# Attention items of two heads with both kinds of attention, row-paired score and maxima matmuls, and softmax division moved to the last stage

## The reference

```python
qkv = x @ qkv_w + qkv_b                              # q, k, v of 16 heads x 16 channels
std_logits = q . k * 16 ** -0.5                      # kind DOT
write_lines = exterior(x_prev @ w1_write, x @ w2_write)   # 6 numbers per head, unit length
read_lines = exterior(x @ w1_read, x @ w2_read)
geo_logits = (read_lines . J write_lines) * inc_scale     # kind GEO, 6 channels
std_out = softmax(causal(std_logits)) @ v
geo_out = softmax(causal(geo_logits)) @ (x @ geo_w + geo_b)
gate = mean(sigmoid(x @ gate_w + gate_b))
x = layernorm(x + ((1 - gate) * std_out + gate * geo_out) @ out_w + out_b)
x = layernorm(x + (silu(x @ w_gate) * (x @ w_up)) @ w_down)   # hidden 768, int weights / 127
```

## Time and profile before

| | us |
|---|---|
| median of 3 runs (lowest, highest) | 2109.17 (2107.64, 2111.22) |
| span of the profiled execution | 2112.1 |
| stage project / attend / finish in it | 241 / 1525 / 346 |
| busy PE, ACT, DVE, POOL | 1930.6, 1273.4, 1129.4, 336.9 |

### The profile page before, as it was taken

The page is one execution under the profiler, slowest core; times in us unless marked ns, Lnnn a source line. Parts: engine busy times, 40 slices in busy tenths (PEclk is TensorE's granted clock), DMA queues, the critical chain, the costliest instruction groups (busy, mean ns, idle before and its releaser), DMA issues. The chain is left out here.

```text
span 2112.1 us, 35917 instructions
## 1 busy us (share of the span) xinstructions
PE 1930.6 (91%) x11400; PEld 769.0 (36%) x11400; DVE 1129.4 (53%) x2179; ACT 1273.4 (60%) x1641; POOL 336.9 (16%) x609
## 2 busy tenths in 40 slices
PE   8888498999998999999899999989999995899998
PEld 4444122333332333333233333323333322556555
DVE  5666377565564655556465655646565403443442
ACT  4555544577776777677677767767777783222121
POOL 3333303111211110111111011111101111000000
PEclk9999699999999999999999999999999997999999
DMA  6668660404133250414324041432500004112000
GB/s 192 205 211 254 163 107 25 86 21 90 37 70 46 50 86 6 91 20 73 49 47 86 6 91 21 72 46 50 86 6 30 4 11 103 43 51 65 20 20 20
DMA packets 138525, 145.83 MB, mean 69 GB/s; under 512 B 46784, under 2 KB 120768, under 8 KB 136288
## 3 DMA queue, kind: packets, MB, share of 16 engines
q1 hardware_dynamic: 137136, 140.32, 30.4%
q0 software_dynamic: 624, 2.75, 0.4%
q10 hardware_dynamic: 576, 0.28, 0.1%
HBM read 88.25 MB, written 54.53 MB: 68 GB/s over the span
## 5 line engine op out<-in xcount | busy, mean ns | idle before, releaser
L931 ACT ACTIVATE prob<-ex 128x1024 f32<-128x1024 f32 (+2 forms) x1280 | 1074.5, 893 | 444.4 <-PE ex L776 438.8
L946 DVE TENSOR_REDUCE mp<-mx 128x1 f32<-128x512 f32 (+3 forms) x1280 | 749.2, 609 | 547.4 <-PE mx L794 287.5
L776 PE MATMUL ex<-qa,ka 98*128 98x512 bf16 (+3 forms) x2560 | 675.6, 354 | 62.7 <-issue 28.3
L827 PE MATMUL pv<-prob,va 128*32 128x512 f32 (+3 forms) x5120 | 613.4, 552 | 7.6 <-POOL prob L752 7.3
L791 PE MATMUL mx<-ka,qa 96*128 96x512 bf16 (+3 forms) x1280 | 450.1, 353 | 14.7 <-DVE mp L946 13.8
L752 POOL TENSOR_SCALAR_AFFINE_SELECT prob<-prob 128x256 f32<-128x256 f32 x512 | 205.8, 408 | 1288.3 <-ACT prob L931 1287.8
L776 PEld LDWEIGHTS ex<-qa,ka 98*128 98x128 bf16 x2560 | 200.2, 99 | 474.3 <-ACT prob L931 306.3
L791 PEld LDWEIGHTS mx<-ka,qa 96*128 96x128 bf16 x1280 | 123.7, 97 | 340.4 <-DVE mp L946 239.1
L827 PEld LDWEIGHTS pv<-prob,va 128*32 128x32 f32 x5120 | 101.7, 108 | 206.7 <-issue 181.8
L1291 ACT ACTIVATE sg<-pg 128x512 f32<-128x512 f32 x48 | 28.7, 597 | 185.6 <-PE pg L1213 185.5
L794 PE MATMUL mx<-mask_qk,ident 128*128 128x128 bf16 x512 | 113.1, 221 | 0.0
(11 more groups left out here) (101 smaller groups left out, 964.7 us busy)
## 6 DMA issues: line engine op xcount, KB each, us to landing
parts<-sp SPq DMA_DIRECT2D x64, 384.0 KB, 3.3
qa<-parts SPq DMA_DIRECT2D x192, 128.0 KB, 6.7
ka<-parts SPq DMA_DIRECT2D x192, 128.0 KB, 8.6
values<-vn SPq DMA_DIRECT2D x64, 256.0 KB, 3.3
va<-values SPq DMA_DIRECT2D x16, 1024.0 KB, 13.8
heads<-on SPq DMA_DIRECT2D x64, 128.0 KB, 1.9
att<-heads SPq DMA_DIRECT2D x64, 128.0 KB, 3.0
xc<-in_xt SPq DMA_DIRECT2D x8, 513.0 KB, 4.2
```

The costliest lines, as they stand in the source:

```text
L776: last = pe.matmul(dst, ka[which][0:NROWM, h, kb * P:(kb + 1) * P], qa[which][0:NROWM, h, (qt + 1) * CH - w:(qt + 1) * CH], start=True, st ...
L827: last = pe.matmul(pv[h * VW:(h + 1) * VW, qt % 2, CH - w:CH], va[kind][:, kb, h * VW:(h + 1) * VW], prob[(s * HG + h) % 8][:, at[j]:at[j] ...
L931: act.activation(prob[n % 8][:, 0:w], ex[:, n % 2, 0:w], ACT.Exp).then_inc(ex_done, 1)
L946: v.tensor_reduce(out=mp[kind][:, h * NKB + qb, k0 // CH:k0 // CH + 1], in_=mx[:, u % 2, 0:w], axis=AX.X, op=ALU.max).then_inc(mx_free[kin ...
```

## The change

Nine things change.

1. An item is now two heads with both kinds. There are still 16 items and 20 steps, but a step is one or two groups (a key block of 512 columns; the last two diagonal blocks share a group): 36 groups per item. Each group has a GEO unit and a DOT unit, each two heads wide; ACT takes exp of one unit (72 per item instead of 80, same columns).
2. GEO is no longer padded: a head's queries stand in 36 + 2 rows, head 0 at partition 0 and head 1 at partition 64. Its two score matmuls use different row halves of the array and write different PSUM banks. DOT stays on the whole array (98 rows, and 128 for head 1).
3. DOT maxima use the four main products only (64 rows), head 0 at partition 0, head 1 at partition 64, again in different halves and banks. The ring `mx` has three banks, so `pv` has one instead of two.
4. The mask of diagonal maxima is added by DVE in a `tensor_tensor_reduce`, not by a matmul.
5. Maxima of item n+1 are spread over item n; those of item 0 are computed before the first item starts. The branch for wide GEO maxima is skipped once per item instead of once per pair.
6. The row maxima are written by eight DMAs of 16 partitions instead of two of 64.
7. The values carry 16 columns of ones. What leaves `attend` is undivided and untransposed (`raw`): `turn` and `normalise` go.
8. `project` has 6 row blocks per chunk instead of 8, and loads the operands of items 0 and 1. POOL writes constant rows of the operand sets (`fix_rows`, six memsets per set; the third set's stand at the start of `attend`, and PE waits for them).
9. In `finish`, DVE inverts the denominators (`inverse`, 2048 elements per partition and chunk), POOL multiplies by the gate and the values (`weigh`, four operations), DVE adds the two kinds straight into `mix_t`. The transposes and ACT's copy of the mix go. The sigmoid of the gate moves into the last item of `attend`.

```diff
-HG = 4
-ITEMS = 2 * NPAIR
+ITEMS = B * PAIRS_OF_HEADS
+MX_RING = 3
...
 def load_operands
+        if side == 0 and not minor:
+            src = parts[kind][0, b, slot + piece, bass.ds(first, n), :].unsqueeze(0).to_broadcast([2, n, T])
+        else:
+            src = parts[kind][side, b, slot:slot + 2, bass.ds(first, n), :]
...
+def fix_rows(g, to, fixed, done):
+    g.memset(dk[96:98, 0, :], 1.0).then_inc(fixed, 1)
...
+    for a in range(2):
+        g.wait_ge(fixed, done + 4 + a)
+        g.memset(gk[HALF * a + 32:HALF * a + 64, :], 1.0).then_inc(fixed, 1)
...
 rows (SP)
-                for i in range(2):
-                    q.dma_start(qa[which][NROW + i:NROW + i + 1, :, :].rearrange("p h (k t) -> p (h k) t", t=P),
-                                mrow[:, i, :]).then_inc(m_in, 16)
+                for a in range(2):
+                    for i in range(2):
...
+                        for kind, dst in ((GEO, geo), (DOT, dot)):
+                            n = (2 * kind + a) * NKB
+                            q.dma_start(dst.rearrange("p (k t) -> p k t", t=P),
+                                        mrow[n:n + NKB, i, :]).then_inc(m_in, 16)
...
 scores (PE)
+                for kb, w in groups[j]:
+                    for a in range(2):
+                        if kind == GEO:
+                            rows = slice(HALF * a, HALF * a + GEO_FULL)
+                            lhs, rhs = k_set[rows, kb * P:(kb + 1) * P], q_set[rows, (qt + 1) * CH - w:(qt + 1) * CH]
+                        else:
+                            rows = slice(0, DOT_FULL[a])
...
+                        last = pe.matmul(ex[:, n % 2, a * CH + at:a * CH + at + w], lhs, rhs, start=True, stop=True)
...
+            def max_pair(nxt, u):
...
+                for a in range(2):
+                    t = 2 * u + a
+                    if t >= MX_RING:
+                        pe.wait_ge(mx_free, nit * NTILE + t + 1 - MX_RING)
+                    rows = slice(HALF * a, HALF * a + DOT_MAIN)
+                    pe.matmul(mx[:, t % MX_RING, 0:w], q_set[rows, a, qb * P:(qb + 1) * P],
+                              k_set[rows, a, k0:k0 + w], start=True, stop=True).then_inc(mx_ready, 1)
...
 step (PE)
+                for j in range(groups):
+                    scores(it, which, s, j, GEO, head)
+                    some(j)
+                    scores(it, which, s, j, DOT, head)
+                    if j == groups - 1:
+                        some(groups)
+                    if j == 0 and s == MT_STEP and nxt:
+                        max_rows(nxt)
+                    earlier(j)
+                for j in range(groups, 2):
+                    earlier(j)
...
 max_pair (DVE)
+                    if on_diagonal:
+                        last = v.tensor_tensor_reduce(
+                            out=dull[:, t % MX_RING, 0:w], in0=mx[:, t % MX_RING, 0:w], in1=mask_qk[:, CH - w:CH],
+                            scale=1.0, scalar=3 * MASKED, op0=ALU.add, op1=ALU.max, accum_out=to)
...
 finish
+            def inverse(c, par):
+                v.wait_ge(att_in[par], (c // 2 + 1) * 9 * 16)
+                v.reciprocal(den[par][:, :, :, :], den[par][:, :, :, :]).then_inc(inv_ready, 1)
...
+            def weigh(c, par):
+                g.wait_ge(inv_ready, c + 1)
+                for kind in ((DOT,) if head else (GEO, DOT)):
+                    g.tensor_tensor(out=den[par][:, kind, :, :], in0=den[par][:, kind, :, :],
+                                    in1=gb[par][:, kind, :].unsqueeze(1).to_broadcast([P, NK, CH]), op=ALU.mult)
+                    g.tensor_tensor(out=att[par][:, kind, :, :], in0=att[par][:, kind, :, :],
+                                    in1=den[par][:, kind, :, :], op=ALU.mult).then_inc(part_ready, 1)
...
                     if m == 2 and has_mix:
-                        mixed(c + 2, par, False)
+                        inverse(c + 2, par)
...
+                if has_mix:
+                    mixed(c + 2, par, False)
                 add_up(c, par, SECOND, not has_second)
...
+            first_inverse()
+            inverse(1, 1)
             mixed(0, 0, True)
-            mixed(1, 1, False)
             add_up(0, 0, FIRST, True)
...
+            mixed(1, 1, True)
             round_(0, 0, True, True, False, True)
```

More of the change, by code:

```diff
@@ L249, in project @@
         wide_ready = sem("wide_ready")
-        ones_in = sem("ones_in")
         dve = sem("dve")
@@ L911, in _ @@
[L911 to L919 removed]
+                        wide_pair(nxt, u)
+                pe.wait_ge(negm_ready, nxt[0] + 1)
+                pe.transpose(mx[:, (NMX - 1) % MX_RING, 0:P], negm[:, :], ident[:, :]).then_inc(mx_ready, 1)
@@ new lines, in times_v @@
+            def times_v(it, which, use, s, j, head):
+                qt, groups = STEPS[s]
+                if s in DIAGONAL:
+                    pe.wait_ge(masked, it * NMASK + MASK_AT[s, j, DOT] + 1)
+                else:
+                    pe.wait_ge(ex_done, it * NEX + UNIT_AT[s, j, DOT] + 1)
+                if s == 0 and j == 0:
+                    pe.wait_ge(sets[which]["v_in"], (use + 1) * 16)
+                if s == FIRST_OF[qt] and j == 0 and not (head and qt == 0):
+                    pe.wait_ge(on_ready, it * NQT + qt)
+                at = 0
+                for kb, w in groups[j]:
+                    for blk in range(NBLK):
+                        kind, a = blk // 2, blk % 2
+                        last = pe.matmul(pv[blk * VW:(blk + 1) * VW, CH - w:CH],
+                                         sets[which]["v"][:, kb, blk * VW:(blk + 1) * VW],
+                                         prob[UNIT_AT[s, j, kind] % NPROB][:, a * CH + at:a * CH + at + w],
+                                         start=kb == 0, stop=kb == TT * qt + TT - 1, tile_position=(0, blk * VW))
+                    at += w
+                last.then_inc(pv_done, 1)
@@ new lines, in step, with earlier @@
+            def step(at, before, nxt, s, head):
+                it, which, use = at
+                places = shares(s) if nxt else [[] for _ in range(1 + len(STEPS[s][1]))]
+                groups = len(STEPS[s][1])
+                def some(i):
+                    for u in places[i]:
+                        max_pair(nxt, u)
+                def earlier(j):
+                    prev, ps = (at, s - 1) if s else (before, NSTEP - 1)
+                    if prev is not None and j < len(STEPS[ps][1]):
+                        times_v(*prev, ps, j, head)
+                for j in range(groups):
[9 more added lines that the diff above has]
+                    earlier(j)
@@ new lines, in item @@
+            def item(at, before, nxt, head):
+                it, which, use = at
+                pe.wait_ge(sets[which]["geo_in"], (use + 1) * LOADS * 16)
+                pe.wait_ge(m_in, (it + 1) * 128)
+                for s in range(NSTEP):
+                    step(at, before, nxt, s, head)
+                    if s == 3 and isinstance(it, int) and it == LAST_ITEM:
+                        pe.wait_ge(gate_ready, 4)
+                        pe.transpose(mx[0:NC * TT, 0, 0:P], gate[:, :], ident[:, :]).then_inc(gate_turned, 1)
@@ L921, in _ @@
+            for it in range(ITEMS - 3, ITEMS):
+                item(static(it), static(it - 1), static(it + 1) if it < LAST_ITEM else None, False)
+            times_v(*static(LAST_ITEM), NSTEP - 1, 0, False)
         @block.scalar
@@ L1026, in _, with finish @@
+            for u in range(NMT):
+                max_pair(0, u)
+            max_rows(0, True)
+            item(0, True, True)
+            with v.Fori(1, ITEMS - 1) as it:
+                item(it, False, True)
+            item(ITEMS - 1, False, False)
             take(ITEMS - 1, NQT - 1, False)
-            normalise(ITEMS - 1, NQT - 1, False)
-def finish(nc, x, heads, gate_z, ident, weights, out):
+def finish(nc, x, raw, gates, ident, weights, out):
     NT = NC * TT
```

920 lines of the change are left out of this document (447 added, 473 removed).

## The result

The changed kernel takes 2443.72 us (median of 4 runs, 2441.62 to 2452.76) against 2109.08: a ratio of 1.159 (1.157 to 1.162), slower by 16%, where I had said 2022 and faster. The profiled execution has a span of 2443.3 us.

The account below looks back on a forecast made before the run. TensorE was taken to bound the attention, and to be the busy engine in the last stage. From 2112.1, attention -139, projection -20 and last stage +72 gave 2025 profiled, 2022 timed; range for all 1880 to 2130, own range 1960 to 2090.

Parts of the forecast that it names:

- Item of 83: Attention, steady part: an item takes 83 us, from 72.2 of TensorE work plus waits; bounds 75 to 91.
- the branch: Attention: skipping the wide-maxima branch once per item costs TensorE 2.7 us.
- the second pair of maxima: Attention: its second tile waits about 0.35 us for a bank, seven times an item: 2.5 us.
- the last groups: Attention: after each 512 queries' last group, TensorE waits 0.75 us for ScalarE, four times an item: 3 us.
- the row maxima: Attention: their eight DMA issues and landing outlast TensorE's 5.6 us of work; wait 1 to 2.3, taken as 1.7.
- my low bound: Attention: 75 us an item if switching into the whole array is free and the waits fall into one another.
- Switches, pairs, masked reductions: Attention: switching from row halves costs 0.09 us, paired halves run at once, masked reductions cost 0.59 per 512 columns like plain ones.
- The rivals on rows: Attention, paired row halves: not running at once gives 2208 us (7%); partial overlap gives 2100 to 2115 (8%).
- Lead of 68: Attention head: memsets 11, first item's maxima 46, branch 2.7 and row maxima 8 take 68 us before the first score.
- Projection -20: Projection: two fewer row blocks save 25 us over eight chunks, 5 given back for item 1's loads; range -27 to +5.
- Last stage +72: Last stage: reciprocal waits +52, slow clock +10, head +22, transposes gone -12; range +40 to +95.
- the VectorE rival: Attention: masked reductions cost twice plain ones and VectorE holds the ring; 90 us an item, 2130 us in all, 11%.

Follow-up runs that it names:

- experiment 5: Changed kernel with operand loads' rows outermost and the previous item's last store issued ahead of the 24 loads: 2029.6 us, ratio 0.9615 to the kernel before the change.
- after: The changed kernel itself, all nine changes against the kernel before, without follow-up edits: 2443.72 us, ratio 1.159.
- experiment 1: Changed kernel with only the order of the operand loads' source dimensions changed, rows outermost: 2108.8 us, ratio 1.0006 to the kernel before the change.

## Why the prediction was wrong

By its own steps:

- **Operand loads: no term.** This is the step that failed. The attention part of the sum prices TensorE, ScalarE and VectorE and has nothing for the 24 loads of each item; the projection part says of the loads of item 1 "I give 5 back". Both took it that a load is hidden as in the earlier trace rows, where the DMA share is 0.31. Measured: 53 us in the projection (275.1 against 221.7) and 285 in the attention (1717 against 1431.8) for the two engines, and 79 more (1352.5) for the order of the queue, in which the last store stands behind the loads. (The store's own 5.3 us on two engines is in that wait too, and no run separates it.) I had asked which engine is late and not what VectorE's copy waits for and what is queued on SyncE ahead of that.
- **Item of 83.** With the loads right, 78.7 in two of three items and 80.3 on average (363.8 to 1327.1 over 12). By terms, of the 78.7: the branch was charged 2.7 and costs 0.2; the second pair of maxima 2.5, and the whole wait for VectorE is (11.6 + 3.5) us in 15 items, 1.0; the last groups 3, and TensorE's wait for ScalarE is 12.8 / 15 = 0.9; the row maxima 1.7, and cost 2.1 in such an item. That is 2.5 + 1.5 + 2.1 - 0.4 = 5.7 less than the sum's 83.6, so 77.9; the 0.8 up to 78.7 is not taken apart. These rows of experiment 5, attention, carry it:

```profile
PE ex L836 <- DMA dq<-mrow: 39.8, 13, 7.1
...
PE ex L836 <- ACT prob L982: 12.8, 46, 0.5
PE mx L857 <- DVE mp L1010: 11.6, 50, 0.6
...
PE mx L857 <- DVE mp L1006: 3.5, 11, 0.3
```

  The 7.1 in the first is the lead's. The terms that I had bounded from VectorE's and ScalarE's latencies were too large; that the waits fall into one another, as my low bound said, is likely and not shown.
- **Switches, pairs, masked reductions.** As forecast: 0.10 on leaving the halves, pairs at once, a masked tile of 512 at about 0.61 from start to start. The rivals on rows and on VectorE's reduction are out.
- **Lead of 68.** In "after" 275.1 to the first score at 341.0: 66.
- **Projection -20.** -19 with the loads spread (241 to 221.7).
- **Last stage +72; measured +105.** The reciprocal (12.94, forecast 13.4) and TensorE's wait before the sixth piece are right: 47.7 in six rounds against 52. Three terms were short. The clock after that wait: the piece takes 5.1 to 6.45 in the six rounds (2132.91 to 2139.36 below) instead of 3.43, 14.3 in all, and in three rounds `down` starts slow as well (12.0 to 12.3 for 48 instructions instead of 10.6), 4.8; 19 instead of 10. GpSimd's products and VectorE's normalising: "nothing", and TensorE waits 20.6 before `down`, where it waited 5.5 before the change. The head: the first output product comes 48 after the stage's first load instead of 42, as the inputs landed at 17.5 instead of some 13. 9 + 15 + 6 = 30, against the 33 that were missing.

```profile
2132.91 3.78 PE L1301 MATMUL pg<-y_t,wg_f 128*128 128x512 f32 x4 [7.95 <-DVE ht L1460]
...
2139.36 1.04 PE L1266 MATMUL pt<-ident,y 128*128 128x128 f32 x8
2143.52 3.72 PE L1317 MATMUL po<-wd_f,ht 128*128 128x256 f32 x16 [3.12 <-DVE ht L1460]
```

- **The range** ended at 2130 since each bound came from an engine's list. (By its own terms, 7 more in 15 items and 13 in the lead, the VectorE rival came to 2140.) None of the rivals was a DMA, though the change rewrites every operand load. That experiment 5 comes to 2029.6, close to 2022, does not save the forecast: its attention is 33 us below my sum (1352.5 against 1386) and its last stage 36 above (453.7 against 418), and the two make up for each other.

## What to carry to other kernels

When a change rewrites a load, read the order of its dimensions as well as its bytes: the size of the outermost one on either side can set how many DMA engines take part, and a load that starts early may still hold a store that an engine needs. List for every engine that waits what stands ahead, on the issuing queue, of the transfer that it waits for. And a long operation on VectorE costs by its length at one place more than by its sum: the same reciprocals in eight pieces, with GpSimd's work moved away from VectorE's, took 72 us less in the last stage (453.7 to 381.6); no run separates the two.

## What was not expected of the hardware

- Loads with an outer dimension of 2 had 2.0 packets of 4 KB under way at a time and moved 12.5 packets per us; with rows outermost 40 per us for 16 rows and 14 for 6 rows (experiment 1), those of the kernel before 34.8.
- A store with an outer dimension of 2 took 5.3 us for 128 packets of 2 KB; one of the kernel before took 0.5 for 128 packets of 1 KB.
- An issue on SyncE's queue behind them took up to 2.4 us in the item shown (0.59 for a row-maxima DMA), so the queue itself is held up.
- VectorE's operations from SBUF to SBUF ran one for one with GpSimd's: four of 0.41 in 9.42 us. `ht`, which reads PSUM and `sg`, took 0.63 to 0.69 beside the same products, no longer than alone.
- Two matmuls of 512 columns in the two row halves take the time of one, 0.22, at 38 rows and at 64 rows (0.32 there, with the 0.10 of leaving the halves).
